# A decoder layer on one core: an outsized step size at chunk starts in place of cleared banks, and a new order of all pieces

## What is computed

```python
delta = jax.nn.softplus(dlt @ W_dt.T + b_dt)
A = -jnp.exp(A_log)
dA = jnp.exp(jnp.einsum('bld,dn->bldn', delta, A))
dBu = jnp.einsum('bld,bln,bld->bldn', delta, Bm, u)
# chunks of CHUNK = 64 tokens, each with carry = 0 at its start
carry = a * carry + bu          # step over the tokens of a chunk
y = jnp.einsum('bkdn,bkn->bkd', carry, c)
y = y * jax.nn.silu(res)
```

## Time and profile before

| | us |
|---|---|
| median of 3 runs | 2794.74 |
| lowest, highest | 2792.72, 2795.35 |
| the profiled execution, its own time | 2792.28 |
| its span in the trace | 2790.5 |
| its granted TensorE clock, mean share | 0.955 |
| busy: PE, DVE, ACT, POOL | 2424.6, 2140.0, 1802.9, 2074.5 |

### The profile page before, as it was taken

How to read it: one execution, slowest core, us unless ns; L and a number is a source line. 1 busy time by engine, 2 the same in 40 slices (tenths; PEclk the granted TensorE clock), 3 DMA queues, 4 the chain that set the end, 5 groups by cost and what they waited for, 6 DMA issues and landing times. The chain is left out here.

```text
span 2790.5 us, 49779 instructions
## 1 busy us (share of the span) xinstructions
PE 2424.6 (87%) x14816; PEld 1660.6 (60%) x14816; DVE 2140.0 (77%) x3586; ACT 1802.9 (65%) x3972; POOL 2074.5 (74%) x968
## 2 busy tenths in 40 slices
PE   3578888888889898889889888898888879999998
PEld 2345666666666666666666666666665545555554
DVE  1778999999999999999999999999999832322332
ACT  1666777877888888777877787878777541211111
POOL 2999999999999999999999999999999500000000
PEclk8788999999999999999999999999998879999999
DMA  3456566666666666666666666666666360343221
GB/s 118 128 133 149 150 165 168 165 158 157 157 169 166 160 158 165 165 162 168 166 169 164 162 164 166 165 173 163 166 172 158 86 180 12 91 126 96 78 79 31
DMA packets 319323, 399.65 MB, mean 143 GB/s; under 512 B 115697, under 2 KB 256241, under 8 KB 314962
## 3 DMA queue, kind: packets, MB, share of 16 engines
q1 hardware_dynamic: 303698, 384.91, 53.5%
q10 hardware_dynamic: 15360, 11.55, 1.5%
HBM read 300.86 MB, written 94.37 MB: 142 GB/s over the span
## 5 line engine op out<-in xcount | busy, mean ns | idle before, releaser
L506 POOL TENSOR_TENSOR arena<-arena 128x1024 f32<-128x1024 f32 x512 | 1208.2, 2363 | 66.6 <-DMA arena<-w_dram 42.3
L582 ACT ACTIVATE dA_ps<-arena,a_neg 128x252 f32<-128x252 f32 x2048 | 868.7, 461 | 330.4 <-DVE dA_ps L787 172.0
L764 DVE TENSOR_TENSOR_SCAN arena<-dA_ps,arena 128x512 f32<-128x512 f32 x672 | 803.6, 1208 | 112.5 <-ACT dA_ps L582 88.0
L516 POOL TENSOR_TENSOR arena<-arena 128x1024 f32<-128x1024 f32 (+1 forms) x416 | 808.1, 1943 | 17.8 <-DVE arena L764 17.2
L764 DVE TENSOR_TENSOR_SCAN dA_ps<-dA_ps,arena 128x512 f32<-128x512 f32 x352 | 416.2, 1205 | 3.9 <-POOL arena L506 3.7
L887 PE MATMUL a_ps<-xT,w_conv 128*128 128x256 f32 x1536 | 369.8, 391 | 0.0
L829 DVE TENSOR_REDUCE mx<-s_ps 128x2 f32<-128x512 f32 x497 | 334.0, 672 | 23.2 <-PE s_ps L887 23.2
L887 PEld LDWEIGHTS a_ps<-xT,w_conv 128*128 128x128 f32 x1536 | 288.4, 194 | 54.1 <-issue 16.5
L887 PE MATMUL y_ps<-arena,sel 128*32 128x256 f32 x4096 | 257.5, 393 | 55.5 <-DVE m_rows L835 27.8
L640 ACT ACTIVATE probs<-st_ps 128x512 f32<-128x512 f32 x493 | 285.3, 579 | 29.7 <-PE st_ps L887 25.5
L887 PE MATMUL s_ps<-k_st,q_st 96*128 96x256 f32 x994 | 260.6, 344 | 43.7 <-DVE mx L829 28.0
(11 more groups left out here) (111 smaller groups left out, 3272.9 us busy)
## 6 DMA issues: line engine op xcount, KB each, us to landing
arena<-delta_dram SPq DMA_DIRECT2D x512, 128.0 KB, 2.8
arena<-w_dram SPq DMA_DIRECT2D x512, 128.0 KB, 3.2
arena<-bc_dram SPq DMA_DIRECT2D x128, 256.0 KB, 4.5
q_st<-q_parts_dram SPq DMA_DIRECT2D x512, 64.0 KB
k_st<-k_parts_dram SPq DMA_DIRECT2D x512, 64.0 KB
w_dram<-u SPq DMA_DIRECT2D x32, 512.0 KB, 2.8
delta_dram<-delta SPq DMA_DIRECT2D x32, 512.0 KB, 3.8
k_parts_dram<-parts SPq DMA_DIRECT2D x32, 512.0 KB, 4.0
```

Of the source, the lines that this page charges most:

```text
L506: pool.tensor_tensor(dBu[:, n % NB], w_r[:, n // RP % 2, t % RP].unsqueeze(1).to_broadcast([P, QS, L]), bc_r[:, b.par, 0], ALU.mult).then_ ...
L516: pool.tensor_tensor(h[:, n % NH, states], h[:, n % NH, states], bc_r[:, b.par, 1, states], ALU.mult).then_inc(s_hC, 1)
L582: last = nc.scalar.activation(dA[n % NDA][:, q, :, 1:], delta_r[:, n // (2 * RP) % 2, t % RP].rearrange("p (c t) -> p c t", t=CH)[:, :, 1: ...
L764: nc.vector.tensor_tensor_scan(dst, decays, dBu[:, n % NB, 2 * half:2 * half + 2].rearrange("p q t -> p (q t)"), 0.0, ALU.mult, ALU.add).t ...
```

## The change

Four things change together.

- After `w_piece`, POOL writes CUT = 1e20 into delta at the first token of each chunk (128 partitions x 16 elements), and raises a new semaphore `s_cut`. `delta_store` waits for it. exp(A * 1e20) with a negative A is zero, so `decay` writes all 256 elements, and neither the zeroing of the banks at the start nor `clear_starts` is there any more. A bank whose half is multiplied on DVE is free for ACT as soon as that product is done; the semaphore of the half is raised by its scan.
- HC_DVE has 10 halves in place of 11, others than before. POOL multiplies 22: 8 whole tiles and 6 single halves.
- The lists of `run_steps` are in another order on every engine, and a few offsets differ.
- At the start the bias rows are loaded first and converted on ACT, and for the first batch the gate projection and its silu come after softplus (`first_gate`).

```diff
+CUT = 1e20
-HC_DVE = [(1, 0), (1, 1), (4, 1), (5, 0), (5, 1), (6, 1), (8, 0), (9, 1), (10, 0), (10, 1), (14, 1)]
+HC_DVE = [(2, 1), (3, 1), (4, 1), (5, 0), (8, 0), (8, 1), (9, 1), (10, 0), (10, 1), (14, 1)]
...
+            for tile, name in bias_parts:
+                sp.dma_start(tile, io[name]).then_inc(s_bias_ld, 16)
             sp.dma_start(w_xc.rearrange("p q t -> p (q t)"), io["w_xc"]).then_inc(s_conv_ld, 16)
             sp.dma_start(conv_rows, io["conv_rows"].partition_broadcast(P)).then_inc(s_conv_ld, 16)
-            for tile, name in bias_parts:
-                sp.dma_start(tile, io[name]).then_inc(s_bias_ld, 16)
...
             def delta_store(b):
-                wait_all(sp, (s_delta, 2, b, 2), *[(s, 128, b.back(2), 128) for s in s_rep])
+                wait_all(sp, (s_cut, 1, b, 1), *[(s, 128, b.back(2), 128) for s in s_rep])
...
             run_steps([
-                (O_K - 2, load_ctx),
-                (O_Q + 3, store_parts(q_dram, s_q_hi, s_q_lo, s_q_dram)),
                 (O_REP + 13, replicate(3)),
...
-                (O_SP + 2, w_store),
-                (O_OUT, load_x_tok),
-                (0 + 1, load_x),
-                (O_SP + 2, delta_store),
-                (O_XP + 2, bc_load),
-                (O_REP + 1, replicate(0)),
-                (O_REP + 7, replicate(2)),
-                *[(O_LD + HG * gr - 2, load_stack(gr)) for gr in range(NG)],
-                (O_X2T + 3, load_columns),
+                (O_Q + 3, store_parts(q_dram, s_q_hi, s_q_lo, s_q_dram)),
+                (O_REP + 7, replicate(2)),
+                (O_K + 5, store_parts(k_dram, s_k_hi, s_k_lo, s_k_dram)),
+                (O_XP + 2, bc_load),
+                (O_K - 2, load_ctx),
+                (O_REP + 1, replicate(0)),
+                (O_SP + 2, delta_store),
+                (O_OUT - 1, load_x_tok),
+                (O_X2T + 5, load_columns),
+                (0 + 1, load_x),
+                (O_SP + 2, w_store),
+                *[(O_LD + HG * gr - 1, load_stack(gr)) for gr in range(NG)],
                 (O_X2T + 3, store_x2T),
                 (O_REP + 6, replicate(1)),
             ], B)
...
                 pool.tensor_tensor(u[:], u[:], delta[:], ALU.mult).then_inc(s_w, 1)
+                pool.wait_ge(s_w, b.value(1, 1))
+                starts = delta[:].rearrange("p k (c t) -> p k c t", t=CH)[:, :, :, 0:1]
+                nc.gpsimd.memset(starts, CUT).then_inc(s_cut, 1)
...
                     if n >= NDA:
-                        act.wait_ge(s_scan[(n - NDA) % 2], (n - NDA) // 2 + 1)
+                        b_was, rest = divmod(n - NDA, 2 * NU)
+                        was = divmod(rest, 2)
+                        if was in HC_DVE:
+                            act.wait_ge(s_hC_v, len(HC_DVE) * b_was + HC_DVE.index(was) + 1)
+                        else:
+                            act.wait_ge(s_scan[was[1]], NU * b_was + was[0] + 1)
                     for q in range(2):
                         last = nc.scalar.activation(
-                            dA[n % NDA][:, q, :, 1:],
-                            delta_r[:, n // (2 * RP) % 2, t % RP].rearrange("p (c t) -> p c t", t=CH)[:, :, 1:],
-                            ACT.Exp, scale=a_neg[:, t, 2 * half + q:2 * half + q + 1])
+                            dA[n % NDA][:, q], delta_r[:, n // (2 * RP) % 2, t % RP], ACT.Exp, scale=a_neg[:, t, 2 * half + q:2 * half + q + 1])
                     last.then_inc(s_dA, 1)
...
+                (O_SP + 2, first_gate),
...
-                (O_Q + 1, high(s_q_mm, s_q_hi, s_k_dram, 0)),
+                (O_Q, high(s_q_mm, s_q_hi, s_k_dram, 0)),
...
-            for i in range(NDA):
-                nc.vector.memset(dA[i][:], 0.0).then_inc(s_const_v, 1)
...
-            def clear_starts(t, half):
-
-                def piece(b):
-                    state = dA[(2 * b.value(NU, t) + half) % NDA]
-                    dve.wait_ge(s_hC_v, b.value(len(HC_DVE), HC_DVE.index((t, half)) + 1))
-                    nc.vector.memset(state[:, :, :, 0:1], 0.0).then_inc(s_scan[half], 1)
-                return piece
```

More of the change, by code:

```diff
@@ L261, in bank @@
             return ctx.enter_context(nc.psum_tensor(name, shape, F32))
-        dA = [bank(f"dA_ps{i}", [P, 2, NCH, CH]) for i in range(NDA)]
+        dA = [bank(f"dA_ps{i}", [P, 2, L]) for i in range(NDA)]
         y_ps = bank("y_ps", [P, L + P])
@@ L530, in _ @@
             act.wait_ge(s_bias_ld, 16 * len(bias_parts))
+            act.wait_ge(s_const_v, N_ROWS)
+            nc.scalar.activation(bias[:], rows, ACT.Copy).then_inc(s_const_a, 1)
             nc.scalar.activation(a_neg[:], a_neg[:], ACT.Exp).then_inc(s_const_a, 1)
@@ L551, in silu, with first_gate, later_gate_evac, piece @@
                 nc.scalar.activation(u[:], u[:], ACT.Silu).then_inc(s_u, 1)
-                act.wait_ge(s_gate, b.value(2, 2))
-                nc.scalar.activation(gate[:, b.par], gate[:, b.par], ACT.Silu).then_inc(s_gsilu, 1)
+                if b.back(1):
+                    silu_gate(b)
                 nc.scalar.preload_act_table_set(EXP_LN)
+            def first_gate(b):
+                if not b.back(1):
+                    for half in range(2):
+                        gate_evac(half)(b)
+                    silu_gate(b)
+                    nc.scalar.preload_act_table_set(EXP_LN)
+            def later_gate_evac(half):
+                def piece(b):
+                    if b.back(1):
+                        gate_evac(half)(b)
+                return piece
             def xp_evac(b):
@@ L703, in _ @@
                 (O_SILU, silu),
-                *[(O_GATE + 4 * half + 2, gate_evac(half)) for half in range(2)],
+                *[(O_GATE + 4 * half + 2, later_gate_evac(half)) for half in range(2)],
                 (O_K + 1, high(s_k_mm, s_k_hi, s_q_dram, 1)),
@@ L918, in gate_proj, with first_gate, later_gate, piece @@
                 return piece
+            def first_gate(b):
+                if not b.back(1):
+                    for m in range(ND):
+                        gate_proj(m)(b)
+            def later_gate(m):
+                def piece(b):
+                    if b.back(1):
+                        gate_proj(m)(b)
+                return piece
             def x_proj(b):
+                if not b.back(1):
+                    pe.wait_ge(s_front, 16 * len(front_weights))
+                    pe.wait_ge(s_const_v, N_SET)
                 pe.wait_ge(s_u, b.value(1, 1))
@@ L940, in piece @@
                     n = b.value(NU, 4 * m)
+                    if m == 0 and not b.back(1):
+                        pe.wait_ge(s_const, 16 * N_WEIGHTS)
+                        pe.wait_ge(s_const_p, 4)
                     pe.wait_ge(s_hC, b.value(len(HC_POOL), sum(t < 4 * m + 4 for t in HC_POOL)))
```

83 lines of the change are left out of this document (43 added, 40 removed).

## The result

| | before | after |
|---|---|---|
| median of the runs, us | 2795.05 (4 runs, 2792.72 to 2797.99) | 2827.59 (4 runs, 2824.60 to 2832.01) |
| ratio to before | 1 | 1.0117 (95%: 1.0100 to 1.0135) |
| profiled execution, us | 2792.28 | 2832.01 |

The changed kernel is 32.5 us slower; 2821 was predicted. The profiled execution is the longest of the four, 4.4 us above the median, so differences between the two traces come out at 39.7 us and not at 32.5.

The account below looks back on a forecast made before the run. POOL's work plus its waits was taken to bound the batches. +45.8 - 23.3 + 20.2 - 16.0 = +26.7 us on 2792.28 gave 2819.0, as a median 2821; forecast 2808 to 2835 (chance 0.42), range 2774 to 2850.

Parts of the forecast that it names:

- Part 1: POOL's own work in each batch: one half more, +39.4 us, and writing CUT, +6.4, all on its path; +45.8.
- Part 2: Clearing of banks by DVE: POOL's dBu no longer waits for it, -23.3 us, bounds 0 and -23.3.
- Rival D: At POOL's dBu: the clearing's 23.3 us come back as waits for scans; +50 us, time 2844; chance 0.12.
- Part 3: Stores and replication of w: w and delta reach the waiting tile later, 0.65 us a batch, +20.2; bounds -30.3 and +81.
- Both slips: Before `replicate(0)`: later store issued about 1.0 us later behind load_stack(3); `load_ctx` about 0.6 later through ACT's copy of q.
- rival C: SP's queue: stores wait behind the stack's bytes, 2.0 to 2.6 us a batch; +68 us, time 2863; chance 0.07.
- Part 4: Start of the run: gate work and weight wait leave the path to softplus, -16.0 us, between -11 and -18.
- What would show it: Signs in POOL's and SP's rows: POOL some 46 us busier, no bank waits, w waits 1.5 us or more.

Follow-up runs that it names:

- b_cut_hc10: The kernel before with CUT in place of the clearing and the changed kernel's ten halves on DVE, old orders and start: 2771.9 us, ratio 0.9904.
- b_cut: The kernel before with CUT in place of the clearing alone, eleven halves on DVE, old orders and start: 2777.6 us, ratio 0.9942.
- b_cut_hc10_start: The changed kernel with every engine's list of the kernel before, keeping CUT, ten halves and the new start: 2755.9 us, ratio 0.9856.
- b_best_late3: The changed kernel with all orders of the kernel before, but load_stack(3) one slot later, ahead of the stores: 2809.4 us, ratio 1.0052.
- a_sp: The changed kernel with SP's whole list of the kernel before, other engines' lists new: 2785.2 us, ratio 0.9967.
- a_sp_act: The changed kernel with SP's and ACT's lists of the kernel before, PE, DVE and POOL new: 2754.8 us, ratio 0.9853.

## Why the prediction was right, and where its steps were not

The time was right by a sum whose two largest terms were both wrong as prices of their parts, by some 50 us each, in opposite directions. That they cancel is luck: nothing in the prediction ties them together.

| term | predicted | measured |
|---|---|---|
| one half more on POOL | +39.4 | -11 (b_cut_hc10), -4 (with the new start), +1, 0 |
| CUT written, clearing gone | +6.4 - 23.3 = -16.9 | -16 (b_cut), -18 (with the new start) |
| w and delta later (order) | +20.2 | +73 (all lists), of it SP 42 and then ACT 32 |
| start | -16.0 | -18, -20, -13 |
| sum | +26.7 | +33 |

The parts along b_cut, b_cut_hc10, b_cut_hc10_start and the changed kernel add up: -16 - 11 - 13 + 73 = +33.

Read as an account of POOL's time in the two traces, the rows came nearly as written: work +40.0 us (45.8 said), waits for a bank -23.3 (-23.3), for w +28.2 (+20.2), for a scan -6.2 and for delta +6.3 (none), first dBu -14.7 (-16.0). But such an account doesn't price the parts: take one away, and the waits change with it.

**Part 1, the half: the failed step.** "All of it is on POOL's path, nothing covers it." POOL's busy time did rise as written (+40.0 for +45.8). But I had added POOL's work to POOL's waits as if the waits were fixed. In the kernel before, the leg before w_piece holds 48.0 us of work and takes 49.25, so it has room for the half's 1.23; from 400 to 2000 the waits in it are 0.62 us a batch for a bank, 0.16 for delta, 0.14 for w and 0.12 for a scan. And the earlier trace rows had the sign of it: 28 waits for delta of at most 0.3 us. POOL came to w_piece nearly every time when delta was just done, so ACT set that start, and what POOL did before it was free up to those waits. With CUT only 0.7 us of room is left there; what pays for the rest is the second leg, and why delta is ready 0.65 us sooner after the first dBu with the new list (DVE's product gone, or the other tiles) stays open. The write of CUT was right: w's start to the next dBu is 1058.06 - 1055.48 = 2.58 us, some 0.25 more than a pitch of 2.33 (predicted 0.2).

**Part 2, the clearing: right in the net.** 23.3 us went, and 9.4 came back, 3.0 as waits for scans and 6.4 on the delta row, which I had at nothing; the waits for w fell by 6.2, which I hadn't either. The net of CUT and clearing is -16 us (-7 to -23) against -16.9. Rival D, that all of it returns as waits for scans, did not happen: 3.0 us did.

**Part 3, the order: right in mechanism, too small.** Both slips named were there. `load_stack(3)` ahead of the stores: I took the issue time alone, 1.0 us, and held the landing at under 4.65 us "if in as much again". The issue was right: the later store goes out 1.60 us behind w_piece's end in place of 0.55 (medians). The landing was the missing piece: of the later store it is 3.8 us before (delta) and 6.5 after (w). The term is rival C's, 2.0 to 2.6 us a batch; b_best_late3 shows 55 / 31 = 1.8. The copy of q ahead of the exp: I took its own 0.588 us, where ACT's list cost 1.4 us at v. ACT also stands at it until PE has q, 0.4 us more in a batch, and v's projection itself is slower (last section). My reason for taking 0.65, that `load_ctx`'s bound "holds whatever the stores do", was wrong: `replicate(0)` waits for the later of two things, and a bound from one of them is a lower bound.

**Part 4, the start: right.** -14.7 us at the first dBu against -16.0. x_proj's eight matmuls took 3.25 us there against 1.97 before, which is as much as was missed. All of it was kept.

**What would show it.** POOL +40 us busy (46 said), no wait of dBu on a bank, 58.5 us of waits for w over 31 batches, which is 1.9 each (1.5 or more said), `replicate(0)` 10.8 us after w (8 or more), first w at 41.05 (near 40): all as written. None of them could have told that the half was free, because busy time rises whether or not it costs.

**Not settled.** In the profiled executions the experts start 108.3 us after POOL's last product, before 100.6. In the five others with all lists old it was 100.2 to 106.0, in b_best_late3 109.4, and in the six others with new lists 104.9 to 112.1. So the new orders seem to cost some us there too, but not `load_columns` alone, which is back in its old place in the 104.9, the 106.6 and the 112.1.

## What to carry to other kernels

Before you price work added to the busiest engine, look at what it waits for at the next point where it takes data from another engine: many short waits there are a sign that the other engine sets the time, and that work up to the length of the idle time before that point may be free. Here 36 us of work took the place of 42 us of waits; only a run without the part gives its price. Where an issue waits for several things, price each and take the latest; and for a store that others wait for, count the bytes issued ahead of it on the same queue, not only its own issue time.

## What the runs showed of the hardware

The store's landing, above: 2.7 us alone, 5.9 behind 0.5 MB of other transfers of the same queue, whose packets start first. The other is TensorE's clock in the middle of a run. In a_sp, the windows in which q's projection runs behind 1.21 us of idle PE:

```profile
1036.00:1037.00 1.00, 0.59 (x2) 0.38 (x3) 1.00 (x3) 0.98 (x3) 1.00 (x1) 1.00 0.90 221
1037.00:1038.00 1.00, 1.00 (x3) 0.77 (x3) 1.00 (x3) 1.00 (x1) 1.00 (x2) 0.54 1.01 254
```

The granted clock falls from 1.00, the 2.4 GHz level, to 0.54 and then 0.50, the 1.2 GHz level, from 1038 to 1040, once PE works again. The eight matmuls of q, a_sp, PE in order of time:

```profile
1036.41 0.46 PE L906 MATMUL a_ps<-bias 4*128 4x512 f32 x1 [1.21 <-ACT delta L600]
1036.80 3.55 PE L906 MATMUL a_ps<-x1T,w_q 128*128 128x256 f32 x8
```

and a_sp_act, where the clock stays at 1.00 there:

```profile
1089.75 0.47 PE L906 MATMUL a_ps<-bias 4*128 4x512 f32 x1 [1.21 <-ACT delta L600]
1090.15 1.99 PE L906 MATMUL a_ps<-x1T,w_q 128*128 128x256 f32 x8
```

The idle time just before is the same 1.21 us in both, and PE was busy 4.57 us of the six before (1030 to 1036, and 1083 to 1089), so neither tells the two apart; where the clock falls, q is 1.6 us later, just where ACT waits for it. Over the run v's projection shows it (busy us in all, mean ns of one), a_sp and then a_sp_act:

```profile
L906 PE MATMUL f_ps<-w_v,ctxT 128*128 128x256 f32 x256 | 87.0, 499 | 0.0
```

```profile
L906 PE MATMUL f_ps<-w_v,ctxT 128*128 128x256 f32 x256 | 72.4, 432 | 0.0
```

PE is busy with them 87.0 - 72.4 = 14.6 us longer, 0.46 us in each of the 32 batches, a third of the 1.4 us by which v is later there.
